# Rows taken from SBUF by one-hot products: two of 16 columns, in bf16, instead of one in f32

## The chip, the cores and the metric

One core of one Trainium2 chip runs the kernel. The metric is the device time of one execution in microseconds. The engines named below are TensorE (PE; PEld are its weight loads), VectorE (DVE), ScalarE (ACT), GpSimd (POOL), SyncE (SP) and the DMA engines.

## The reference

Four graph layers run over the same 6,250 nodes of 128 features and the same 100,000 edges (`src`, `dst`, sorted by `dst`), with `x = layernorm(x + layer(x))` after each:

```
L0: xl = x@W_lin + b; alpha = edge softmax over src of leaky(s_i[src] + s_j[dst]); sum over dst of alpha * xl[src]
L1: sum over dst of edge_weight * x[src]; out = x + sum; relu(out@W1 + b1)@W2 + b2
L2: per (edge type, dst) softmax of 4 scores, averaged; sum over dst of attn * (x[src] @ W_r[type]); layernorm, relu
L3: h = x@W; edge softmax over dst of leaky(s_src[src] + s_dst[dst]), own loops; sum over dst of alpha * h[src]
```

What matters here is the step that all four share: for every edge, fetch the row of its source node, weigh it, and add it up by target.

## The kernel before

Edges are padded to 128 x 784: each of the 128 partitions owns 784 consecutive edges ("columns"). A node's row lives at partition p, block b (node = 50p + b, `NB` = 50 blocks). Each layer has one **pass** over the 784 columns: layers 0, 1 and 2 in `sum_strands` (name prefixes l0z, l1z, l2z), layer 3 in `sum_messages` (l3z). A pass is cut into 48 full turns of 16 columns and two half turns of 8. For a turn:

- POOL issues one indirect DMA for each column (line 1103, line 927 in layer 3); it fetches 128 rows from the table in DRAM into `rows`, a ring of six turns (`RING`). The list of row numbers, `idx`, is in SBUF. POOL waits for `weighed` of six turns before.
- One column of each full turn in layers 0, 1 and 3 isn't fetched but **picked** (class `Picks`). PE makes the source numbers of the column into a row that all partitions see (`pcode`, in PSUM, line 822). DVE compares it with the names of a partition's nodes (`pnames`, in SBUF), and writes f32 one-hot matrices, one of 128x128 for each of the 50 blocks (line 813, in two or three parts). PE multiplies each with the node rows in SBUF and sums over the 50 blocks in `pfound` (line 836). ACT copies the result into `rows` (line 847). Everything about a pick is done one turn ahead: DVE marks the next turn's pick at the head of a turn.
- DVE then waits for the turn's DMAs and for its pick, weighs the rows into `msg`, and adds them up step by step, each step waiting for the last: four steps of two tensor operations (lines 1068 and 1069) in layers 0 to 2, 16 steps of one operation (line 899) in layer 3.
- SP stores the running sums to `prefix` in DRAM.

`Residual0` is extra DVE work in turns 20 to 32 of layer 0. Between passes stand the tails (`tail0` to `tail3`): POOL fetches 50 x 128 sums from `prefix`, DVE and ACT normalize them, SP writes the next table. Several operands of DVE (`keep`, `kept`, `factors`, `pcode`, `msg` in layer 3) are in PSUM, so that its frequent operations have one input in SBUF and one in PSUM.

The order of work on each engine is written out by hand; semaphores carry it from engine to engine.

```
WIDTH, RING, ACCS = 16, 6, 2
self.nc.vector.tensor_tensor(self.hot[i][:, 0:hi - lo], bc_mid(self.code[:], hi - lo), bc_last(self.names[:, lo:hi], P), ALU.is_equal)
mm = self.nc.tensor.matmul(self.found[:], self.hot[i][:, b - lo], self.nodes[:, b], start=b == 0, stop=b == NB - 1)
```

Of the kernel before, what the change touches and what calls it, by code (L numbers as in the profile page):

```python
# [755 lines left out]
WIDTH, RING, ACCS = 16, 6, 2  # L756
# [4 lines left out]


# [19 lines left out]
def halved(hot):  # L782
    return [hot[:, 0:NB // 2], hot[:, NB // 2:NB]]


class Picks:
# [3 lines left out]
    def __init__(self, nc, s, g, nodes, hot, columns):  # L790
        self.nc, self.g, self.nodes, self.hot, self.columns = nc, g, nodes, hot, columns
        self.count, self.parts, at = len(columns), [], 0
        for piece in hot:
            self.parts.append((at, min(at + piece.shape[1], NB)))
            at += piece.shape[1]
        self.base, self.names = s.sb("pbase", [P, 1]), s.sb("pnames", [P, NB])
        self.code, self.found = s.ps("pcode", [P, P]), s.ps("pfound", [P, nodes.shape[2]])
        self.coded, self.hotted, self.summed, self.placed = (s.sem("p" + n) for n in ("coded", "hotted", "summed", "placed"))

    def start(self, chain):  # L800
        v = self.nc.vector
        chain(v.tensor_scalar(self.base[:], self.g.part[:], float(NB), None, ALU.mult))
        chain(v.tensor_scalar(self.names[:], self.g.iota[:, 0:NB], self.base[:, 0:1], None, ALU.add))

    def on_vector(self, eng, k):
        if k >= self.count:
            return
        eng.wait_ge(self.coded, k + 1)
        n = len(self.parts)
        for i, (lo, hi) in enumerate(self.parts):  # L810
            if k:
                eng.wait_ge(self.summed, n * (k - 1) + i + 1)
            self.nc.vector.tensor_tensor(self.hot[i][:, 0:hi - lo], bc_mid(self.code[:], hi - lo), bc_last(self.names[:, lo:hi], P),  # L813
                                         ALU.is_equal).then_inc(self.hotted, 1)

    def landed(self, eng, k):
        if k < self.count:
            eng.wait_ge(self.placed, k + 1)

    def name(self, k):  # L820
        j = self.columns[k]
        self.nc.tensor.matmul(self.code[:], self.g.src[:, j:j + 1].to_broadcast([P, P]), self.g.ident[:],  # L822
                              start=True, stop=True).then_inc(self.coded, 1)

    def on_tensor(self, pe, k):
        if k >= self.count:
            return
        if k == 0:
            self.name(0)
        else:  # L830
            pe.wait_ge(self.placed, k)
        n = len(self.parts)
        for i, (lo, hi) in enumerate(self.parts):
            pe.wait_ge(self.hotted, n * k + i + 1)
            for b in range(lo, hi):
                mm = self.nc.tensor.matmul(self.found[:], self.hot[i][:, b - lo], self.nodes[:, b], start=b == 0, stop=b == NB - 1)  # L836
            mm.then_inc(self.summed, 1)
        if k + 1 < self.count:
            self.name(k + 1)

    def on_scalar(self, act, k, slot, weighed):
        if k >= self.count:
            return
        act.wait_ge(self.summed, len(self.parts) * (k + 1))
        if k >= RING:
            act.wait_ge(weighed, k - RING + 1)
        self.nc.scalar.copy(slot, self.found[:]).then_inc(self.placed, 1)


def sum_messages(nc, name, g, order, table, prefix, width, weigh, aside, spot):  # L850


    with Space(nc, name) as s:
# [11 lines left out]
        picks = Picks(nc, s, g, *spot, [hi - 1 for lo, hi in BATCHES if hi - lo == WIDTH])  # L865

        def landed(k):
            return 16 * sum(BATCHES[m][1] - BATCHES[m][0] - (m < picks.count) for m in range(k % RING, k + 1, RING))
# [6 lines left out]
        with s.block() as block:  # L875
            @block.vector
            def _(eng):
# [6 lines left out]
                picks.on_vector(eng, 0)  # L884
                for k, (lo, hi) in enumerate(BATCHES):
                    c = k % ACCS
                    aside.on_vector(eng, chain, k)
                    picks.on_vector(eng, k + 1)
# [16 lines left out]
            @block.tensor  # L905
            def _(pe):
                for k in range(len(BATCHES)):
                    picks.on_tensor(pe, k)
                    aside.on_tensor(pe, k)

            @block.scalar
            def _(act):
                picks.on_scalar(act, 0, rows[:, 0, WIDTH - 1], weighed)
                for k, (lo, hi) in enumerate(BATCHES):
                    aside.on_scalar(act, k)
                    w.on_scalar(act, k, hi - lo)
                    picks.on_scalar(act, k + 1, rows[:, (k + 1) % RING, WIDTH - 1], weighed)

            @block.gpsimd
            def _(pool):  # L920
                pool.wait_ge(indexed, 1)
                for k, (lo, hi) in enumerate(BATCHES):
# [3 lines left out]
                    for u in range(hi - lo - (k < picks.count)):  # L926
# [66 lines left out]
STRIDE = NC // STRANDS  # L993
ABREAST = WIDTH // STRANDS
# [16 lines left out]
def sum_strands(nc, name, g, order, table, prefix, width, weigh, aside, spot=None, acc=None):  # L1011
# [3 lines left out]
    with Space(nc, name) as s:  # L1015
        rows = s.sb("rows", [P, RING, WIDTH, width])
        msg = s.sb("msg", [P, WIDTH, D])
        acc = s.sb("acc", [P, ACCS, WIDTH, D])[:] if acc is None else acc
        keep, kept = s.ps("keep", [P, STRIDE, STRANDS]), s.ps("kept", [P, STRANDS, D])
# [6 lines left out]
        w = weigh(nc, s, us, es, weighed, rows, msg)  # L1026
        full = sum(hi - lo == ABREAST for lo, hi in TURNS)
        picks = Picks(nc, s, g, *spot, [(STRANDS - 1) * STRIDE + TURNS[k][1] - 1 for k in range(full)]) if spot else None

        def picked(k):  # L1030
            return 1 if picks and k < picks.count else 0
# [8 lines left out]
        with s.block() as block:  # L1040
            @block.vector
            def _(eng):
# [4 lines left out]
                chain(v.tensor_copy(keep[:], by_step(order.keep[:])))  # L1047
                last = by_strand(acc[:, ACCS - 1])[:, :, ABREAST - 1]
                if picks:
                    picks.start(chain)  # L1050
                    picks.on_vector(eng, 0)
                for k, (lo, hi) in enumerate(TURNS):
                    aside.on_vector(eng, chain, k)
                    if picks:
                        picks.on_vector(eng, k + 1)
# [8 lines left out]
                    for u in range(hi - lo):  # L1064
                        if lo + u:
                            eng.wait_ge(summed, lo + u)
                        here = sums(k)[:, :, u]
                        chain(v.tensor_tensor(kept[:], last, bc_last(keep[:, lo + u], D), ALU.mult))
                        v.tensor_tensor(here, kept[:], by_strand(msg[:, 0:STRANDS * (hi - lo)])[:, :, u], ALU.add).then_inc(summed, 1)
                        last = here  # L1070
                eng.wait_ge(summed, STRIDE)
# [3 lines left out]
            def _(pe):  # L1075
                for k in range(len(TURNS)):
                    if picks:
                        picks.on_tensor(pe, k)
                    aside.on_tensor(pe, k)

            @block.scalar
            def _(act):
                if picks:
                    picks.on_scalar(act, 0, rows[:, 0, WIDTH - 1], weighed)
                for k, (lo, hi) in enumerate(TURNS):
                    aside.on_scalar(act, k)
                    w.on_scalar(act, k, STRANDS * (hi - lo))
# [1711 lines left out]
```

## Time and profile before

| | us |
|---|---|
| median of 3 runs | 6681.86 (6681.67 to 6683.09) |
| span of the profiled execution | 6678.7 |
| pass of layer 0: first gather to last operation of DVE | 1370.3 to 2297 |
| pass of layer 1 | 2389.1 to 3312 |
| pass of layer 2 | 4453.7 to 5460 |
| pass of layer 3 | 5628.3 to 6551 |

The span leaves 3.2 us to the median. "Busy" is the time in which an engine ran an instruction; for PE the ends are modelled, so the pace is read from counts in a window. An f32 matmul shows as two records on PE and two on PEld. PEclk is the granted TensorE clock as a share of 2.4 GHz; its two levels are 1.2 and 2.4 GHz.

### The profile page before, as it was taken

The numbers are of one execution on the slowest core, as the hardware profiler recorded it, in microseconds if no ns is written. First come the engines' busy times: TensorE is split into PE (matmuls) and PEld (weight loads), VectorE is DVE, ScalarE is ACT, GpSimd is POOL, SyncE is SP. The second block draws the span as 40 slices with busy tenths as digits, with TensorE's granted clock in tenths as the row PEclk, the third lists the DMA queues.
The fourth block names the chain that finished last, engine by engine and source line by source line (L and its number), as shares of the span: only waits on it lengthen the run. The fifth ranks groups of instructions, "written<-read, shape, count | busy, mean of one in ns | idle before, by whom it ended". The sixth has DMA issues, their size and how long they took to land. (4 is left out here: it accounts for less than half of the span.)

```text
span 6678.7 us, 61345 instructions
## 1 busy us (share of the span) xinstructions
PE 3332.5 (50%) x21638; PEld 2959.0 (44%) x21638; DVE 5046.5 (76%) x7174; ACT 1003.4 (15%) x2297; POOL 4583.7 (69%) x4753
## 2 busy tenths in 40 slices
PE   7530117467777457777468857730000004777770
PEld 5530106357777457777443327730000003777770
DVE  8999998778898677787647779986343446888886
ACT  1013333200000010000034435520000003000002
POOL 0027777677777677777667777777777767777774
PEclk9999558788989778888779988865555556888885
DMA  3036011134444344444339974433343332333332
GB/s 60 1 148 256 2 32 18 26 85 115 115 112 113 101 115 110 110 110 110 99 124 345 343 283 122 126 88 107 103 108 104 103 92 59 112 112 112 112 112 71
DMA packets 588107, 763.09 MB, mean 114 GB/s; under 512 B 118267, under 2 KB 479585, under 8 KB 568345
## 3 DMA queue, kind: packets, MB, share of 16 engines
q1 hardware_dynamic: 416916, 375.57, 17.7%
q0 software_dynamic: 152672, 272.57, 17.1%
q10 hardware_dynamic: 18210, 111.02, 4.2%
q8 instruction: 171, 2.80, 0.2%
q14 instruction: 138, 1.13, 0.1%
HBM read 346.63 MB, written 412.16 MB: 114 GB/s over the span
## 5 line engine op out<-in xcount | busy, mean ns | idle before, releaser
L1103 POOL DMA_INDIRECT l2z_rows<-proj,l2z_idx x784 | 764.5, 975 | 246.2 <-issue 238.6
L2685 POOL DMA_INDIRECT l2s_krow<-table_k,l2s_idx x762 | 721.8, 947 | 232.2 <-issue 230.4
L1103 POOL DMA_INDIRECT l0z_rows<-table,l0z_idx x736 | 697.3, 947 | 234.7 <-issue 224.0
L927 POOL DMA_INDIRECT l3z_rows<-table,l3z_idx x736 | 694.6, 944 | 234.7 <-issue 224.0
L1103 POOL DMA_INDIRECT l1z_rows<-table,l1z_idx x736 | 694.6, 944 | 233.5 <-issue 213.0
L836 PE MATMUL l3z_pfound<-l3h_hn,l3h_hot 128*128 128x130 f32 x4800 | 645.1, 303 | 233.9 <-DVE l3h_hot L813 233.9
L836 PE MATMUL l1z_pfound<-g_x,l2o_xT 128*128 128x128 f32 x4800 | 638.3, 303 | 238.9 <-DVE l2o_xT L813 238.9
L836 PEld LDWEIGHTS l3z_pfound<-l3h_hn,l3h_hot 128*128 128x128 f32 x4800 | 637.2, 218 | 241.8 <-issue 234.7
L836 PEld LDWEIGHTS l1z_pfound<-g_x,l2o_xT 128*128 128x128 f32 x4800 | 630.5, 218 | 246.6 <-issue 239.0
L2097 POOL DMA_INDIRECT first_sj<-scores,first_atdst x504 | 504.7, 1001 | 170.7 <-issue 170.7
L836 PE MATMUL l0z_pfound<-first_rows,l0r_hot 128*128 128x140 f32 x3648 | 468.0, 292 | 82.0 <-DVE l0r_hot L813 81.9
L836 PEld LDWEIGHTS l0z_pfound<-first_rows,l0r_hot 128*128 128x128 f32 x3648 | 458.0, 197 | 92.9 <-DVE l0r_hot L813 92.9
L1136 DVE TENSOR_TENSOR l2z_msg<-l2z_rows,l2z_factors 128x1024 f32<-128x1024 f32 (+1 forms) x50 | 60.0, 1200 | 511.5 <-DMA l2z_rows<-proj,l2z_idx 511.0
L2643 PE MATMUL l2s_bank<-l2o_wr,l2o_xT 128*128 128x512 f32 x800 | 373.5, 622 | 98.0 <-ACT l2s_proj L2657 83.2
L813 DVE TENSOR_TENSOR l2o_xT<-l1z_pcode,l1z_pnames 128x3200 f32<-128x3200 f32 x96 | 330.3, 3481 | 20.8 <-PE l1z_pcode L822 20.7
L813 DVE TENSOR_TENSOR l3h_hot<-l3z_pcode,l3z_pnames 128x3200 f32<-128x3200 f32 x96 | 330.4, 3483 | 12.8 <-PE l3z_pcode L822 12.5
L606 POOL IOTA sd_nidi<- 128x50 int32 x1 | 0.2, 170 | 429.8 <-POOLq L60 429.8
L2643 PEld LDWEIGHTS l2s_bank<-l2o_wr,l2o_xT 128*128 128x128 f32 x800 | 153.5, 197 | 317.7 <-issue 167.9
L899 DVE SCALAR_TENSOR_TENSOR l3z_acc<-l3z_acc,l3z_xx,l3z_msg 128x128 f32<-128x128 f32 x784 | 271.8, 347 | 25.9
L2541 PE MATMUL l2s_bank<-l2o_kn,l2o_xT 128*128 128x128 f32 x2200 | 286.2, 299 | 5.3 <-DVE l2o_xT L2522 5.3
L2541 PEld LDWEIGHTS l2s_bank<-l2o_kn,l2o_xT 128*128 128x128 f32 x2200 | 286.3, 216 | 5.5 <-issue 5.5
L268 PE MATMUL sd_turn<-g_ident,prep_key 128*128 128x128 f32 x112 | 27.5, 428 | 493.0 <-DVE prep_key L245 487.7
(619 smaller groups left out, 7639.4 us busy)
## 6 DMA issues: line engine op xcount, KB each, us to landing
proj<-l2s_proj ACTq DMA_DIRECT2D x100, 1024.0 KB
spread_q<-prep_zero SPq DMA_DIRECT2D x98, 656.0 KB
l2s_zrow<-spread_q SPq DMA_DIRECT2D x98, 656.0 KB, 4.8
prefix<-l0z_acc SPq DMA_DIRECT2D x196, 256.0 KB, 3.1
prefix<-l2o_kn SPq DMA_DIRECT2D x196, 256.0 KB
prefix<-l2z_acc SPq DMA_DIRECT2D x196, 256.0 KB
prefix<-l3z_acc SPq DMA_DIRECT2D x48, 1040.0 KB, 4.1
l2z_rows<-proj,l2z_idx POOLq DMA_INDIRECT x784, 2.6
```

Of the source, the lines that this page charges most:

```text
L268: mm = self.nc.tensor.transpose(self.turn[q][:, u], self.keys[at % 2][:, c:c + P], self.g.ident[:])
L606: nc.gpsimd.iota(nid_i[:], pattern=[[1, NB]], base=EP, channel_multiplier=NB).then_inc(numbered, 1)
L813: self.nc.vector.tensor_tensor(self.hot[i][:, 0:hi - lo], bc_mid(self.code[:], hi - lo), bc_last(self.names[:, lo:hi], P), ALU.is_equal).t ...
L836: mm = self.nc.tensor.matmul(self.found[:], self.hot[i][:, b - lo], self.nodes[:, b], start=b == 0, stop=b == NB - 1)
L899: v.scalar_tensor_tensor(acc[:, c, u, 0:D], sum_before(k, u)[:, 0:D], w.factor(k, lo, u), msg[:, u], ALU.mult, ALU.add).then_inc(summed, 1)
L927: nc.gpsimd.indirect_dma_start(out=rows[:, k % RING, u, :], out_offset=None, in_=table, in_offset=bass.IndirectOffsetOnAxis(ap=idx[:, lo + ...
L1103: nc.gpsimd.indirect_dma_start(out=rows[:, k % RING, c * (hi - lo) + u, :], out_offset=None, in_=table, in_offset=bass.IndirectOffsetOnAxi ...
L1136: chain.add(self.v.tensor_tensor(msg[:, 0:half], rows[:, 0:half], bc_last3(factor[:, 0:half], D), ALU.mult))
L2097: nc.gpsimd.indirect_dma_start(out=sj[:, j, :], out_offset=None, in_=g.scores0, in_offset=bass.IndirectOffsetOnAxis(ap=at_dst[:, j:j + 1], ...
L2541: mm = self.nc.tensor.matmul(self.found, self.hot[:, b], self.nodes[:, b], start=b == 0, stop=b == NB - 1)
L2643: mm = nc.tensor.matmul(bank[m % 2][:, b], xT[:, i, :], wr[:, c:c + wide], start=True, stop=True)
L2685: nc.gpsimd.indirect_dma_start(out=krow[:, k % KRING, c * (hi - lo) + u, :], out_offset=None, in_=g.table_k, in_offset=bass.IndirectOffset ...
```

## The change

- In layers 0, 1 and 3 two columns of each full turn, and one of each half turn, are picked: 98 picks in a pass in place of 48, and 686 gathers in place of 736.
- Node rows are held as three bf16 pieces whose sum is the f32 row exactly: the high piece is read in place from the f32 rows (every second bf16), the middle and low piece are made by DVE into a new tile `ml` (class `Pieces`: three DVE operations for each group of blocks). For layer 0 that is done ahead of the pass (`first`, five times ten blocks), for layers 1 and 3 inside `tail0` and `tail2`.
- The one-hot matrices are bf16. ACT turns the row of source numbers into a row of block numbers in bf16 in SBUF (`digit`), and DVE compares `digit` with `blocks` (SBUF, bf16). Parts: two of 25 blocks, in layer 0 four of 12 or 13 blocks. A ring holds four parts (six in layer 0: three reused areas and three new).
- For each block PE runs three bf16 products with the same one-hot matrix. `pfound` is doubled. Everything about picks is two turns ahead (`AHEAD`), and DVE's marks are spread over a turn in five shares, between the steps of the sum.
- `RING` goes from six to four turns, in layer 2 too. `keep`, `kept` and the factors are packed in one PSUM area; `keep` leaves out the last eight steps, which read the copy in SBUF.

```diff
-WIDTH, RING, ACCS = 16, 6, 2
+WIDTH, RING, ACCS, PICKED = 16, 4, 2, 2
+class Pieces:
+    def make(self, chain, b):
+        v, x, rest, ml = self.nc.vector, self.nodes[:, b], self.rest[:, 0:b.stop - b.start], self.ml[:, b]
+        chain(v.tensor_tensor(rest, x, x.bitcast(BF16)[:, :, 1::2], ALU.subtract))
+        chain(v.tensor_copy(ml[:, :, 0], rest.bitcast(BF16)[:, :, 1::2]))
+        chain(v.tensor_tensor(ml[:, :, 1], rest, ml[:, :, 0], ALU.subtract))
+AHEAD = 2
+SHARES = 5
 class Picks:
...
+    def mark(self, eng, at):
+        n, i = at // self.parts, at % self.parts
+        lo, hi = self.cuts[i], self.cuts[i + 1]
+        if i == 0:
+            eng.wait_ge(self.dug, n + 1)
+        if at >= len(self.hot):
+            eng.wait_ge(self.summed, at - len(self.hot) + 1)
+        out = self.hot[at % len(self.hot)].rearrange("p b (r q) -> p b r q", q=16)
+        names = self.blocks[:, lo:hi].unsqueeze(2).to_broadcast([P, hi - lo, P // 16, 16])
+        digit = self.digit[:, n % 2].rearrange("p (r q) -> p r q", q=16).unsqueeze(1).to_broadcast([P, hi - lo, P // 16, 16])
+        self.nc.vector.tensor_tensor(out, names, digit, ALU.is_equal).then_inc(self.hotted, 1)
+    def on_vector(self, eng, k, share):
+        todo = self.of(k + AHEAD)
+        lo, m = todo.start * self.parts, len(todo) * self.parts
+        for at in range(lo + m * share // SHARES, lo + m * (share + 1) // SHARES):
+            self.mark(eng, at)
...
+                for b in range(self.cuts[i], self.cuts[i + 1]):
+                    hot = self.hot[at % len(self.hot)][:, b - self.cuts[i]]
+                    t.matmul(found, hot, high[:, b, 1::2], start=b == 0, stop=False)
+                    t.matmul(found, hot, self.ml[:, b, 0], start=False, stop=False)
+                    mm = t.matmul(found, hot, self.ml[:, b, 1], start=False, stop=b == NB - 1)
+                mm.then_inc(self.summed, 1)
+    def dig(self, act, n):
+        if n == 0:
+            act.wait_ge(self.based, 1)
+        act.wait_ge(self.coded, n + 1)
+        if n >= 2:
+            act.wait_ge(self.hotted, self.parts * (n - 1))
+        self.nc.scalar.activation(self.digit[:, n % 2], self.code, ACT.Identity, bias=self.base[:, 0:1]).then_inc(self.dug, 1)
...
                     for u in range(hi - lo):
+                        if picks:
+                            picks.on_vector(eng, k, 1 + u)
...
+    def first(self, chain):
+        for b in range(0, NB, 10):
+            self.pieces.make(chain, slice(b, b + 10))
...
+                    if i >= 2:
+                        eng.wait_ge(normed, GROUPS[i - 2][-1] + 1)
+                        pieces.make(chain, span(GROUPS[i - 2]))
...
+                    j = i - 5
+                    if j >= 0:
+                        eng.wait_ge(ready, GROUPS[j][-1] + 1)
+                        pieces.make(chain, span(GROUPS[j]))
```

## Rows read from the trace of the kernel before

**Rows 1.** The page, part 1: busy us, share of span, instructions of each engine.
```profile
PE 3332.5 (50%) x21638; PEld 2959.0 (44%) x21638; DVE 5046.5 (76%) x7174; ACT 1003.4 (15%) x2297; POOL 4583.7 (69%) x4753
```
**Rows 2.** Busy time in windows: PE, PEld, DVE, ACT, POOL, then PEclk; passes 0, 1, 3.
```profile
1370.30:2288.30 918.00, 679.87 (x4894) 661.13 (x4894) 779.46 (x855) 25.79 (x97) 694.64 (x734) 0.89 0.46 113
2389.10:3307.90 918.80, 649.90 (x4904) 642.17 (x4904) 720.01 (x595) 12.94 (x49) 694.54 (x736) 0.86 0.41 111
5628.30:6546.00 917.70, 655.50 (x4894) 647.70 (x4894) 769.98 (x1320) 29.84 (x147) 693.68 (x736) 0.86 0.38 110
```
**Rows 3.** The page, part 5: busy us, mean ns | idle before, and its cause; layer 1.
```profile
L1103 POOL DMA_INDIRECT l1z_rows<-table,l1z_idx x736 | 694.6, 944 | 233.5 <-issue 213.0
L836 PE MATMUL l1z_pfound<-g_x,l2o_xT 128*128 128x128 f32 x4800 | 638.3, 303 | 238.9 <-DVE l2o_xT L813 238.9
L813 DVE TENSOR_TENSOR l2o_xT<-l1z_pcode,l1z_pnames 128x3200 f32<-128x3200 f32 x96 | 330.3, 3481 | 20.8 <-PE l1z_pcode L822 20.7
```
**Rows 4.** Groups by line and shape, columns as in rows 3.
```profile
L813 DVE TENSOR_TENSOR l0r_hot<-l0z_pcode,l0z_pnames 128x4864 f32<-128x4864 f32 x48 | 250.3, 5214 | 0.0
...
L1068 DVE TENSOR_TENSOR l1z_kept<-l2o_kn,l1z_keep 128x512 f32<-128x512 f32 x196 | 136.3, 695 | 10.2 <-issue 0.9
...
L899 DVE SCALAR_TENSOR_TENSOR l3z_acc<-l3z_acc,l3z_xx,l3z_msg 128x128 f32<-128x128 f32 x784 | 271.8, 347 | 25.9
...
L337 DVE TENSOR_TENSOR sa_toh<-prep_steps,sa_thib 128x2048 bf16<-128x2048 bf16 x49 | 59.9, 1222 | 4.3 <-PE sa_ttally L346 4.3
...
L338 DVE TENSOR_TENSOR sa_tol<-prep_steps,sa_tlob 128x800 bf16<-128x800 bf16 x49 | 27.9, 570 | 0.0
```
**Rows 5.** Waits in passes 0, 1, 3: us in total, times, longest.
```profile
DVE l0z_a L1159 <- DMA l0z_rows<-table,l0z_idx: 80.2, 41, 9.1
DVE l1z_msg L1136 <- DMA l1z_rows<-table,l1z_idx: 158.3, 44, 10.2
DVE l3z_e L974 <- DMA l3z_rows<-table,l3z_idx: 86.6, 43, 8.7
```
**Rows 6.** Bursts of line 836 (layers 3, 0) and line 346: PE, PEld records, PEclk.
```profile
5911.00:5918.00 7.00, 7.00 (x65) 7.00 (x65) 0.00 (x0) 1.00 0.26 55
1803.00:1811.00 8.00, 8.00 (x69) 8.00 (x69) 0.00 (x0) 1.00 0.33 83
200.20:203.20 3.00, 3.00 (x31) 3.00 (x31) 1.00 0.00 0
```
**Rows 7.** Windows of line 268, f32 transposes: PE, PEld busy (x records), PEclk.
```profile
640.00:750.00 110.00, 9.84 (x40) 7.84 (x40) 0.52 0.06 2
116.00:420.00 304.00, 25.59 (x104) 20.39 (x104) 1.00 0.08 1
```
**Rows 8.** Timeline at the start of pass 1: start us, us, engine, line.
```profile
2392.74 6.89 DVE L813 TENSOR_TENSOR l2o_xT<-l1z_pcode,l1z_pnames 128x3200 f32<-128x3200 f32 x2
2392.82 0.94 POOL L1103 DMA_INDIRECT l1z_rows<-table,l1z_idx  x1 [0.30 <-issue]
```
**Rows 9.** Timeline of layer 2's pass and of the sort's end, columns as in rows 8.
```profile
4476.70 3.42 DVE L2428 TENSOR_TENSOR l2b_bwd<-l_qv,l_attn 128x3136 f32<-128x3136 f32 x1
4477.79 3.15 POOL L1103 DMA_INDIRECT l2z_rows<-proj,l2z_idx  x1 [0.30 <-issue]
...
1025.10 7.08 DVE L2133 TENSOR_TENSOR_SCAN sd_si<-first_sokeep,sd_init,sd_si 128x784 f32<-128x784 f32 x4
...
1028.01 1.44 POOL L2097 DMA_INDIRECT first_sj<-scores,first_atdst  x1 [0.30 <-issue]
1029.76 1.44 POOL L2097 DMA_INDIRECT first_sj<-scores,first_atdst  x1 [0.30 <-issue]
```
**Rows 10.** Windows of tail 0 and tail 2, columns as in rows 2.
```profile
2297.00:2389.00 92.00, 2.98 (x10) 1.94 (x10) 40.42 (x113) 25.80 (x114) 55.59 (x58) 0.50 0.27 83
5460.00:5625.00 165.00, 39.41 (x158) 33.24 (x158) 93.91 (x243) 68.71 (x290) 113.34 (x109) 0.54 0.18 52
```

More of the change, by code:

```diff
@@ L779, in on_tensor, with slots @@
         pass
-def halved(hot):
-    return [hot[:, 0:NB // 2], hot[:, NB // 2:NB]]
-class Picks:
[L790 to L798, printed above, removed]
+def slots(flat, sizes):
+    out, at = [], 0
+    for n in sizes:
+        out.append(flat[:, at:at + n * P].rearrange("p (b q) -> p b q", q=P))
+        at += n * P
+    return out
@@ new lines, with __init__, picked, of @@
+AHEAD = 2
+BANK = 512
+SHARES = 5
+class Picks:
+    def __init__(self, nc, s, g, spot, todo, weighed):
+        self.nc, self.g, self.weighed = nc, g, weighed
+        self.nodes, self.ml, self.hot, self.cuts = spot
+        self.columns = [j for batch in todo for j, _ in batch]
+        self.slots = [u for batch in todo for _, u in batch]
+        self.first = [sum(len(batch) for batch in todo[:k]) for k in range(len(todo) + 1)]
+        self.count, self.parts, self.width = len(self.columns), len(self.cuts) - 1, self.nodes.shape[2]
+        self.base, self.blocks = s.sb("pbase", [P, 1]), s.sb("pblocks", [P, NB, 16], BF16)
+        self.digit = s.sb("pdigit", [P, 2, P], BF16)
+        self.code = s.ps("pcode", [P, BANK])[:, 0:P]
+        self.found = [s.ps(f"pfound{h}", [P, BANK])[:, 0:self.width] for h in range(2)]
+        self.based, self.coded, self.dug, self.hotted, self.summed, self.placed = (
+            s.sem("p" + n) for n in ("based", "coded", "dug", "hotted", "summed", "placed"))
+    def picked(self, k):
+        return self.first[k + 1] - self.first[k]
+    def of(self, k):
+        last = len(self.first) - 1
+        return range(self.first[max(0, min(k, last))], self.first[max(0, min(k + 1, last))])
@@ L816, in landed @@
-    def landed(self, eng, k):
[L817 to L822, printed above, removed]
+        chain(v.tensor_copy(self.blocks[:], bc_last(self.g.iota[:, 0:NB], 16)))
+        v.tensor_scalar(self.base[:], self.g.part[:], -float(NB), None, ALU.mult).then_inc(self.based, 1)
+    def mark(self, eng, at):
[9 more added lines that the diff above has]
+        self.nc.vector.tensor_tensor(out, names, digit, ALU.is_equal).then_inc(self.hotted, 1)
@@ L825, in on_tensor @@
     def on_tensor(self, pe, k):
[L826 to L837, printed above, removed]
@@ L925, in _ @@
                         hold(pool, weighed, k - RING + 1)
-                    for u in range(hi - lo - (k < picks.count)):
+                    for u in range(hi - lo - picks.picked(k)):
                         nc.gpsimd.indirect_dma_start(out=rows[:, k % RING, u, :], out_offset=None, in_=table,
@@ L1025, in sum_strands @@
         stored = [s.sem(f"sto{r}") for r in range(ACCS)]
-        w = weigh(nc, s, us, es, weighed, rows, msg)
-        full = sum(hi - lo == ABREAST for lo, hi in TURNS)
-        picks = Picks(nc, s, g, *spot, [(STRANDS - 1) * STRIDE + TURNS[k][1] - 1 for k in range(full)]) if spot else None
+        w = weigh(nc, s, us, es, weighed, rows, msg, room[:, 4 * BANK - NC:])
+        todo = [[((STRANDS - 1) * STRIDE + hi - 1 - i, STRANDS * (hi - lo) - 1 - i) for i in range(STRANDS * (hi - lo) * PICKED // WIDTH)]
+                for lo, hi in TURNS]
+        picks = Picks(nc, s, g, spot, todo, weighed) if spot else None
         def picked(k):
-            return 1 if picks and k < picks.count else 0
+            return picks.picked(k) if picks else 0
         def landed(k):
```

176 lines of the change are left out of this document (112 added, 64 removed).

## The prediction

> **What bounds the kernel now.** First the page's busy line [rows 1]: no engine is full, so the passes are read one by one. In each of the passes 0, 1 and 3 POOL is busy 694 of 918 us [rows 2], and what is left of it is nearly all "issue" [rows 3]: it waits for nobody. Its pace is the bound: 918.8 us for 735 intervals is 1.250 us for a gather. DVE waits for the gathers' DMAs for 80, 158 and 87 us in passes 0, 1 and 3 [rows 5]; so it is occupied for 838, 760 and 831 us of 918 and is a close second. PE is busy for 650 to 680 us [rows 2] and waits for marks. A full turn takes 15 gathers, 18.75 us. The changed passes gain if POOL keeps its pace with fewer gathers and DVE and PE keep up.
>
> **What is removed.** 50 gathers in each of three passes: 50 x 1.250 = 62.5 us each, 187 us in all, if POOL still sets the end. POOL's pass would be 686 x 1.250 = 857 us.
>
> **DVE's marks.** A mark was f32, 3481 ns for 3200 elements [rows 3], 5214 for 4864 [rows 4]; so 96 marks in passes 1 and 3 (330 us), and 48 x 7.1 = 341 us in pass 0. The nearest rows for a bf16 mark are two bf16 comparisons, both inputs in SBUF, 1222 ns for 2048 elements and 570 for 800 [rows 4]: 0.522 ns an element and 152 ns fixed. 3200 elements are 1.82 us, 1600 (12 or 13 blocks) 0.99. Pass 1 and 3: 196 x 1.82 = 357, +27 us. Pass 0: 392 x 0.99 = 388, +47. DVE's occupation becomes 885, 787 and 858 us in passes 0, 1, 3: level with POOL's 857 in layer 3, above it in layer 0. If the two repeated inputs cost the mode that gives 0.522, the f32 price holds: +352 us in each of passes 1 and 3 and some +370 in pass 0.
>
> **PE's products.** A pick was 50 f32 products, two record pairs each: 65 pairs in 7.00 us in layer 3 (108 ns a pair), 69 in 8.00 in layer 0 (116 ns, 140 columns), PEclk 1.00 [rows 6]. A pair takes as long as 256 columns at 2.4 GHz (107 ns), so the weight load is hidden there. A bf16 product passes its columns once; half a pair is 55 ns, in layer 0 59 ns. A pick is 150 x 55 = 8.25 us plus 0.4 for name and hand-over (two pairs, and as much again), and 98 picks are 848 us; in layer 0 98 x 9.25 = 907. PE runs nearly without pause, so I keep the 2.4 GHz level for it. This is the lower bound: the load must hide under 53 ns of columns instead of 107. The only bf16 products of the trace, line 346, take 3.00 us for 31, 97 ns each with only 50 columns [rows 6]. Their clock column says 1.00, but f32 transposes in that same window take 25.59/104 = 0.246 us of busy time, and in a window at 0.52 also 9.84/40 = 0.246 [rows 7]: line 346 ran at the 1.2 GHz level, and its 50 columns are 42 of the 97 ns. If the remaining 55 ns is a load that can't be hidden, it is 28 ns at 2.4 GHz, or 55 if it doesn't scale: a product takes 82 or 109 ns. Taken: hidden, as in the f32 rows, which are the nearest in column count; those loads are also read with a stride, the new ones aren't.
>
> **What the marks do to POOL.** This is the step on which the forecast turns. The old mark has one input in PSUM (`pcode`) and one in SBUF; a gather issued 0.08 us after such a mark begins takes its 0.94 us [rows 8], and the means of 944 [rows 3] say that all do. The new mark has both inputs in SBUF (`digit`, `blocks`). Lines 2428 and 2133 are operations of DVE with two SBUF inputs. Line 2428 runs from 4476.70 to 4480.12; the same gather instruction begun inside it takes 3.15 us and ends at 4480.94, 0.82 us after it. Under four scans in 7.08 us the gathers follow each other at 1.75 us, one for each scan, not 1.25 [rows 9]. So a gather that begins under such an operation goes on only when it ends. No row shows it for a bf16 one; both bounds are kept: no stall, or this one.
> The Trainium skill, "SBUF — State Buffer", section "Who interferes with whom", says that a DVE instruction with two SBUF inputs contends with a GpSimd instruction that reads SBUF. By that rule the trace agrees, in 3.15 us against 0.94, and it makes no exception for bf16.
>
> **Turn by turn, with the stall.** In layer 1 a mark of 1.82 is followed by one step (two operations of 0.69 to 0.70 [rows 4] and their gaps, 1.45), then the next mark. A gather is released when a mark ends; one more follows 1.25 later, and the third, due at 2.50, meets the next mark, which began at 1.45, and is held until 3.27. Two gathers take 3.27 instead of 2.50: 0.77 lost for each of four marks, 3.1 us in a turn. The turn is 14 x 1.25 + 3.1 = 20.6 us against 18.75: +1.85 x 48 = +89 us. In layer 3 four steps of 0.347 [rows 4] with gaps are 1.5; the cycle is 3.34, the loss 0.84 x 4 = 3.4, the turn 20.9: +2.15 x 48 = +103. PE (17.3 us a turn) and DVE (16.1 and 17.5) are hidden under both. In layer 0 eight marks of 0.99 each meet a gather with 0.99/1.25 chance and hold it half a mark, 0.39 us: 3.1 us a turn at most (20.6, +89), and near nothing where the held gather falls into step, since one goes through between two marks. I take the middle for POOL, below 18.75 to 19; then PE's 907 us decides, and behind it the start: `first` puts 15 operations of 1400 elements (1.6 us each by the f32 slope) ahead of the first mark, 23 us. 907 + 23 + some 16 for the last turns' sums is 946 against 926: +20. In turns 20 to 32 DVE's residual rows come on top (1.4 us), beside PE.
>
> **Tails.** `make` adds three operations to each of 13 groups in `tail0` and `tail2`, 1.4 to 2.1 us a group, 18 to 27 us each. DVE is busy 40 of 92 us in tail 0 and 94 of 165 in tail 2 [rows 10], so most is hidden; the last groups trail, and two of the three operations have two SBUF inputs and hold gathers. I take +6 and +12, between 0 and 27 each.
>
> **At nothing.** ACT's moves of digits and rows: ACT is busy 13 to 30 us of a pass [rows 2]; without that slack each would cost some 0.3 us. The smaller ring: POOL's idle time before a gather is its usual 0.3 us throughout [rows 3], and DVE stays within a turn of it; in layer 2's start DVE comes 94 us after POOL, about the time of 64 gathers with their stalls (bounds 0 and +10). SP's stores are unchanged in number.
>
> **Sum.** 89 + 103 + 20 + 18 = +230 us on 6678.7. The median of the runs is 3.2 above the span; against it: 6682 + 230 = 6912 us.
>
> **Rivals.**
> *Gathers aren't held* (bf16 marks leave POOL alone). Passes 1 and 3 follow POOL and DVE: -62 and -55; layer 0 +20, tails +18: 6603 us, faster. For it: no bf16 row in contact with POOL. Against it: every row with two SBUF inputs. It decides when the loss of a turn falls under 1.25 us, what one gather less gives.
> *Weight loads aren't hidden* (82 ns). 98 x (150 x 0.082 + 0.4) = 1245 us in passes 1 and 3, 98 x (150 x 0.087 + 0.4) = 1318 in pass 0: +327, +327, +400, tails +18: 7750 us. PE then sets the end and POOL's stalls are hidden. It decides from 66 ns on (turns of 20.6). For it line 346, against it the f32 pairs. At 109 ns it would be near 8900.
> The Trainium skill, "TensorE: Matmul & The Clock Gate", section "Back-to-back issue gap", gives about 81 ns for a matmul of 128 columns in a stream of loads and matmuls, and 56 for one by itself. By the first this rival's sum would stand at about the same place; no run so far shows it.
> *Marks at the f32 price.* Passes 1 and 3 at DVE's 1113 and 1183 us, pass 0 at 1210: about 7450.
> *No change*: a shorter stall and a smaller gain meet, 6670 to 6695.
>
> **Chances.** Forecast (gathers held, loads hidden) 0.50; gathers not held 0.20; loads not hidden 0.20; marks at the f32 price 0.04; no change or between 0.06. The forecast's own range is 6850 to 7010 (tails 0 to 54 for 18, layer 0's POOL up to +89). Leaving out either of the larger rivals leaves out over 2 in 10 with the forecast's own tails, so the range takes in both: 6590 to 7760. A time within 0.2% (13 us) is about what a measurement can't tell from no change. Faster 0.21, same 0.04, slower 0.75.
>
> **What would show it.** Mean of a gather in l1z and l3z: 1.15 to 1.2 us if held (3.1 us over 14), 0.94 if not. DVE's marks: 1.82 and 0.99 us. PE's records of line 836 in a burst: 55 to 59 ns apart, or 82. DVE's wait for gathers in pass 1 stays large if POOL sets the end; if PE does, DVE and ACT wait for `pfound` and marks. Wrong would be: gathers at 0.94 with PE at 55 (then it is faster), or turns of 25 us.

## The result, and the profile after

The changed kernel takes 6887.65 us (median of 4 runs, 6883.4 to 6892.2) against 6681.76 for the kernel before beside it; the ratio is 1.0309, 95% interval 1.0297 to 1.0322. It is 206 us slower; the forecast was 230 us slower. The profiled execution has a span of 6881.5 us, 202.8 more than before.

Where the time went is read from the first gather of each pass (first starts of the tiles `l0z_rows` to `l3z_rows`): before 1370.3, 2389.1, 4453.7, 5628.3, end 6678.7; after 1368.6, 2438.0, 4570.1, 5746.8, end 6881.5. So the stretch of pass 0 and tail 0 grew by 50.6 us, pass 1 with what follows by 67.5, pass 2 with tail 2 by 2.1, pass 3 with the end by 84.3, and the start is 1.7 shorter: 202.8.

The page after, part 1; its answer before is [rows 1].
```profile
PE 4117.3 (60%) x51638; PEld 3751.8 (55%) x51638; DVE 5134.1 (75%) x7715; ACT 1129.8 (16%) x2741; POOL 4829.2 (70%) x4603
```
POOL has 150 instructions fewer and is busy for 246 us more. For the gathers that is the story in one line: the work that was taken away from POOL comes back as longer instructions.

Windows of the changed kernel, with the columns of [rows 2]: passes 0, 1, 3, then tails 0 and 2 (those of before are in [rows 10]).
```profile
1368.50:2343.20 974.70, 941.44 (x14894) 939.79 (x14894) 825.96 (x1131) 68.94 (x246) 756.15 (x686) 0.98 0.40 105
2437.90:3430.50 992.60, 894.10 (x14904) 886.40 (x14904) 725.66 (x701) 56.99 (x197) 777.97 (x687) 0.95 0.35 101
5746.70:6757.60 1010.90, 919.54 (x14895) 912.01 (x14894) 778.03 (x1439) 68.72 (x297) 793.00 (x686) 0.96 0.34 98
2343.20:2437.90 94.70, 2.99 (x10) 1.96 (x10) 59.59 (x148) 25.81 (x114) 56.41 (x58) 0.50 0.26 78
5581.20:5746.80 165.60, 40.36 (x160) 33.82 (x160) 114.08 (x278) 68.83 (x290) 114.75 (x109) 0.52 0.17 51
```
In pass 0 PE is busy for 941 of 975 us: its products run from 1395.89 to 2335.95 almost without a pause, so it is full. In passes 1 and 3 it isn't, and POOL is busy for 80 to 100 us more than in [rows 2] with 50 gathers fewer.

Groups of the changed kernel, with the columns of [rows 3] (the old L1103 is L1194 now, L813 is L850, L836 is L884 to L886).
```profile
L999 POOL DMA_INDIRECT l3z_rows<-table,l3z_idx x686 | 793.0, 1156 | 219.5 <-issue 208.7
L1194 POOL DMA_INDIRECT l1z_rows<-table,l1z_idx x686 | 777.1, 1133 | 222.5 <-issue 208.4
L1194 POOL DMA_INDIRECT l0z_rows<-table,l0z_idx x686 | 756.1, 1102 | 219.5 <-issue 208.4
L1194 POOL DMA_INDIRECT l2z_rows<-proj,l2z_idx x784 | 766.2, 977 | 246.1 <-issue 238.5
...
L850 DVE TENSOR_TENSOR l2o_xT<-l1z_pblocks,l1z_pdigit 128x3200 bf16<-128x3200 bf16 x196 | 356.6, 1821 | 26.3 <-PE l1z_pfound L886 13.7 <-ACT l1z_pdigit L895 8.6
L850 DVE TENSOR_TENSOR l3h_hot<-l3z_pblocks,l3z_pdigit 128x3200 bf16<-128x3200 bf16 x196 | 355.5, 1815 | 14.9 <-PE l3z_pfound L886 14.2 <-ACT l3z_pdigit L895 0.4
L850 DVE TENSOR_TENSOR l0r_hot<-l0z_pblocks,l0z_pdigit 128x1664 bf16<-128x1664 bf16 x196 | 200.3, 1022 | 105.5 <-PE l0z_pfound L886 101.0 <-issue 0.4
```
The mean gather was 944 ns in [rows 3]; it is 1133, 1156 and 1102 ns in the changed passes and nearly unchanged in layer 2, which has no marks. The idle time before a gather is still "issue", 0.30 us: POOL still waits for nobody, each gather lasts longer. The marks cost what was forecast, 1.82 us for 3200 elements and 1.02 for 1664 (by the forecast's slope 1.02).

How one gather becomes longer: the timeline of layer 1 in mid-pass (start us, us, engine, line; PE's rows left out).
```profile
2899.25 0.95 POOL L1194 DMA_INDIRECT l1z_rows<-table,l1z_idx  x1 [0.30 <-issue]
2899.38 1.81 DVE L850 TENSOR_TENSOR l2o_xT<-l1z_pblocks,l1z_pdigit 128x3200 bf16<-128x3200 bf16 x1
...
2900.51 1.51 POOL L1194 DMA_INDIRECT l1z_rows<-table,l1z_idx  x1 [0.30 <-issue]
...
2901.11 0.69 DVE L1149 TENSOR_TENSOR l1z_room<-l2o_kn,l1z_room 128x512 f32<-128x512 f32 x1
...
2902.32 0.94 POOL L1194 DMA_INDIRECT l1z_rows<-table,l1z_idx  x1 [0.30 <-issue]
...
2902.44 1.81 DVE L850 TENSOR_TENSOR l2o_xT<-l1z_pblocks,l1z_pdigit 128x3200 bf16<-128x3200 bf16 x1
```
The gather at 2899.25 begins 0.13 us ahead of a mark and takes its usual 0.95. The next, at 2900.51, begins under the mark, which ends at 2901.19; the gather ends at 2902.02, 0.83 after it. Compare [rows 8], where a gather under an f32 mark takes 0.94; in pass 1 of the kernel before, 250 gathers begin under an f32 mark, over 0.15 us ahead of its end, and none takes more than 0.95. It is no single case: in pass 3 of the changed kernel 197 of 686 gathers begin under a mark in this sense, and 196 of them end 0.81 to 0.83 us after the mark. The one left begins 0.02 us after the mark's start and takes 0.95.

### The profile page after: what moved, and what is told of

Its sections match the earlier page's. It is cut to its first block and busy times, and to the rows that moved or that the text cites. A ratio compares the mean times of both kernels' runs of the same rounds, so it can differ in the third digit from the quotient of the medians.

```text
span 6881.5 us, 122899 instructions
## 1 busy us (share of the span) xinstructions
PE 4117.3 (60%) x51638; PEld 3751.8 (55%) x51638; DVE 5134.1 (75%) x7715; ACT 1129.8 (16%) x2741; POOL 4829.2 (70%) x4603
## 5 line engine op out<-in xcount | busy, mean ns | idle before, releaser
L999 POOL DMA_INDIRECT l3z_rows<-table,l3z_idx x686 | 793.0, 1156 | 219.5 <-issue 208.7
L1194 POOL DMA_INDIRECT l2z_rows<-proj,l2z_idx x784 | 766.2, 977 | 246.1 <-issue 238.5
L1194 POOL DMA_INDIRECT l1z_rows<-table,l1z_idx x686 | 777.1, 1133 | 222.5 <-issue 208.4
L884 PE MATMUL l3z_pfound<-l3h_hn,l3h_hot 128*128 128x130 bf16 x4900 | 888.2, 224 | 74.8 <-DVE l3h_hot L850 74.6
L884 PE MATMUL l1z_pfound<-g_x,l2o_xT 128*128 128x128 bf16 x4900 | 861.9, 223 | 82.8 <-DVE l2o_xT L850 82.7
L1194 POOL DMA_INDIRECT l0z_rows<-table,l0z_idx x686 | 756.1, 1102 | 219.5 <-issue 208.4
L886 PE MATMUL l3z_pfound<-l3h_ml,l3h_hot 128*128 128x130 bf16 x4900 | 887.4, 224 | 0.0
L885 PE MATMUL l3z_pfound<-l3h_ml,l3h_hot 128*128 128x130 bf16 x4900 | 887.1, 222 | 0.0
L886 PE MATMUL l1z_pfound<-l1m_ml,l2o_xT 128*128 128x128 bf16 x4900 | 861.3, 222 | 0.0
L885 PE MATMUL l1z_pfound<-l1m_ml,l2o_xT 128*128 128x128 bf16 x4900 | 860.7, 221 | 0.0
L884 PEld LDWEIGHTS l3z_pfound<-l3h_hn,l3h_hot 128*128 128x128 bf16 x4900 | 490.0, 100 | 79.7 <-issue 74.2
L884 PEld LDWEIGHTS l1z_pfound<-g_x,l2o_xT 128*128 128x128 bf16 x4900 | 483.8, 99 | 89.0 <-issue 83.3
L885 PEld LDWEIGHTS l1z_pfound<-l1m_ml,l2o_xT 128*128 128x128 bf16 x4900 | 487.9, 100 | 0.7
L886 PE MATMUL l0z_pfound<-l0r_ml,l0r_hot 128*128 128x140 bf16 x2548 | 482.2, 225 | 0.0
L884 PE MATMUL l0z_pfound<-first_rows,l0r_hot 128*128 128x140 bf16 x2548 | 482.0, 224 | 0.0
L885 PE MATMUL l0z_pfound<-l0r_ml,l0r_hot 128*128 128x140 bf16 x2548 | 481.7, 222 | 0.0
L886 PEld LDWEIGHTS l1z_pfound<-l1m_ml,l2o_xT 128*128 128x128 bf16 x4900 | 480.2, 98 | 0.0
L885 PEld LDWEIGHTS l3z_pfound<-l3h_ml,l3h_hot 128*128 128x128 bf16 x4900 | 479.7, 98 | 0.8
L886 PEld LDWEIGHTS l3z_pfound<-l3h_ml,l3h_hot 128*128 128x128 bf16 x4900 | 479.3, 98 | 0.0
```

The source lines that it names most:

```text
L884: t.matmul(found, hot, high[:, b, 1::2], start=b == 0, stop=False)
L885: t.matmul(found, hot, self.ml[:, b, 0], start=False, stop=False)
L886: mm = t.matmul(found, hot, self.ml[:, b, 1], start=False, stop=b == NB - 1)
L999: nc.gpsimd.indirect_dma_start(out=rows[:, k % RING, u, :], out_offset=None, in_=table, in_offset=bass.IndirectOffsetOnAxis(ap=idx[:, lo + ...
L1194: nc.gpsimd.indirect_dma_start(out=rows[:, k % RING, c * (hi - lo) + u, :], out_offset=None, in_=table, in_offset=bass.IndirectOffsetOnAxi ...
```

## Experiments

The theory, H: a gather that begins under a mark is held until the mark's end + 0.82 us; this sets the end of passes 1 and 3, and PE's 300 products a turn set that of pass 0. The rival, L: PE's rows, twice as many as before and with a ring of 4, come late, DVE waits, and the long gather records are a symptom that costs nothing. For L spoke that DVE's wait for rows in pass 1 had grown from 158 us [rows 5] to 233, and PE's load from 650 to 894 us. Four kernels (one pick, thin marks, one product, marks placed by the rule) ran beside a kernel before of 6680.7 us (median); the other three (one input and the two with layer 0 as before) ran on another chip, beside one of 6689.0. The first four of the kernels below ran once each, so their totals have no interval.

**One pick instead of two.**
```diff
-WIDTH, RING, ACCS, PICKED = 16, 4, 2, 2
+WIDTH, RING, ACCS, PICKED = 16, 4, 2, 1
```


> The changed kernel with one pick a turn instead of two (15 gathers, two marks and 150 products in a turn of passes 1 and 3; four marks in pass 0). Theory H, gathers are held by marks: a mark alone between steps lets the gather that begins u after its start end at its own end + 0.82, so it costs 1.81 + 0.82 - 0.94 - u, with u from 0 to 1.25: 0.44 to 1.69, in the mean 1.06. A turn is 15 x 1.25 + 2 x 1.06 = 20.9 us (19.6 to 22.1), the gathers of pass 1 take 960 to 1080 us from first to last against 987 with two picks, although PE has half the work; mean gather 1.0 to 1.15 us. Rival L, late rows: with two picks, 300 products a turn and a ring of 4, rows from PE come late and the long gather records are a symptom; with half of PE's work passes 1 and 3 return to 919 us. Pass 0: PE falls from 940 to 470 us; its gathers take 930 to 1000 us by H, 920 by L.

It took 6909.2 us. The gathers of pass 1 took 984.2 us from first to last, those of pass 3 1003.1 (987.0 and 1001.7 with two picks), those of pass 0 996.8 (964.9 with two). PE has about half the products (7200 a pass instead of 14700), and yet the gathers of pass 1 are only 3 us shorter and those of the other passes are longer. Two marks that stand alone cost (1031 - 944) x 15 = 1.3 us a turn in layer 1 and (1059 - 944) x 15 = 1.7 in layer 3: inside the bounds of two times 0.44 to 1.69, and under the mean of 2.1. L falls for passes 1 and 3. With these losses the two settings tie in layer 1: 14 x 1.25 + 2.6 = 20.1 us a turn with four marks, 15 x 1.25 + 1.3 = 20.1 with two.

**Thin marks.** Only the first block of each part is compared, after one round of full marks; the kernel leaves out the rest of the one-hot matrices, so its picked rows have no meaning:
```diff
-        lo, hi = self.cuts[i], self.cuts[i + 1]
+        lo, hi = self.cuts[i], self.cuts[i + 1] if at < len(self.hot) else self.cuts[i] + 1
...
-        out = self.hot[at % len(self.hot)].rearrange("p b (r q) -> p b r q", q=16)
+        out = self.hot[at % len(self.hot)][:, 0:hi - lo].rearrange("p b (r q) -> p b r q", q=16)
```


> The changed kernel with marks of one block (128 elements, about 0.22 us) instead of 25 or 12 to 13, after the first round of full ones: most of the marks is left out, PE's products, ACT's moves and the gathers all stay. H: the mean gather goes back to 0.94 to 0.96 us and POOL to 857 us; then PE sets the end of passes 1 and 3: 98 picks of 150 x 57.9 ns = 8.7 us are 851 us and with hand-over 865 to 885 in pass 1, 150 x 60.4 ns = 9.06 us are 888 and with hand-over 890 to 910 in pass 3 (987 and 1002 with full marks). Pass 0 stays at PE's 940 us and some 30 more. In all about 6680 us. L: PE's work and the ring are unchanged, so passes 1 and 3 stay within 15 us of 987 and 1002, about 6870 us.

It took 6646.6 us; the expectation's total of about 6680 was 33 us too high, and its 865 to 885 and 890 to 910 us for passes 1 and 3 were met at the low ends. Windows of its passes 0, 1 and 3:
```profile
1369.20:2343.30 974.10, 941.74 (x14894) 940.08 (x14894) 549.96 (x1131) 70.32 (x246) 659.91 (x686) 0.98 0.41 105
2438.20:3303.00 864.80, 855.74 (x14862) 853.87 (x14862) 427.01 (x695) 56.58 (x196) 651.39 (x687) 0.99 0.43 116
5623.40:6520.50 897.10, 886.17 (x14894) 884.47 (x14894) 483.94 (x1439) 74.24 (x297) 649.59 (x686) 0.99 0.38 111
```
The gathers of pass 1 take 860.5 us and their mean is 948 ns. The account closes: (1133 - 948) ns x 686 = 127 us, and pass 1's gathers were 987.0 - 860.5 = 126.5 us longer with full marks; in pass 3 (1156 - 947) x 686 = 143.4 against 143.3. These windows also give PE's own time, where it is hardly held up by marks: 855.7 us in pass 1, 886.2 in pass 3 and 941.7 in pass 0, where the forecast had 848, 848 and 907. Pass 0 stays at 974 us. This run alone doesn't tell a held gather from a DVE that has 300 us less to do; the one with one input, below, does.

**One product for each block.**
```diff
-                    t.matmul(found, hot, high[:, b, 1::2], start=b == 0, stop=False)
-                    t.matmul(found, hot, self.ml[:, b, 0], start=False, stop=False)
-                    mm = t.matmul(found, hot, self.ml[:, b, 1], start=False, stop=b == NB - 1)
+                    mm = t.matmul(found, hot, high[:, b, 1::2], start=b == 0, stop=b == NB - 1)
```


> The changed kernel with one product for each block instead of three: the second and third pieces are left out of the sum, the marks, the moves and the gathers stay. H: passes 1 and 3 stay within 15 us of 987 and 1002 us, mean gather 1.13 to 1.16 us, since POOL and the marks are as they were. L: PE has a third of its work (290 us a pass) and rows are never late, so passes 1 and 3 fall to 857 to 900 us. Pass 0: if PE's 63 ns a product set its end, it is shorter than 974.5 us, by 5 to 45 us, down to what POOL with its held gathers takes (14 x 1.25 + 1.75 to 3 us a turn, 943 to 1000 us, less the 12 us by which the sums trail at the end).

It took 6916.7 us, 29 more than with all three products. The gathers of pass 1 took 986.7 us and of pass 3 1009.8, as H has it. But pass 0 became longer, 1003.2 us against 974.7, with PE busy for 525 instead of 941; the expectation was missed. Its mean gather is 1147 ns, up from 1102. So in pass 0 two limits lie close together: with thin marks PE's 941 us give 974, and with PE relieved the held gathers give 1003. With both, the held gathers lose less than they do alone, and the time is 974.7. From start to start of every 14th gather, the turns of the changed kernel's layer 0 repeat at 19.17 us, with 1.7 us of holding in each, until the residual rows begin, and are then 20.4 us long for some ten turns; with one product they are mostly 20.1 to 20.4 us throughout. A likely reading is that PE's pace, to which DVE's marks are tied by their wait for PE (101 us in that pass), also fixes where the marks fall on the gathers. It is read from the trace and wasn't tried by itself, and each side is one run.

**One input.** The block names are compared with one number for each partition, so that the operation has one SBUF tensor; the kernel leaves the marks' meaning out:
```diff
-        self.nc.vector.tensor_tensor(out, names, digit, ALU.is_equal).then_inc(self.hotted, 1)
+        self.nc.vector.tensor_scalar(out, names, self.base[:, 0:1], None, ALU.is_equal).then_inc(self.hotted, 1)
```


> The changed kernel with each mark replaced by a comparison of the same bf16 block names with one number for each partition: same output size and place, one tensor from SBUF instead of two; the marks' meaning is left out. H in its narrow form, two SBUF inputs hold a gather: the mean gather in passes 1 and 3 goes back to 0.94 to 0.97 us and their length to PE's pace, as with thin marks: gathers of pass 1 860 to 880 us, of pass 3 860 to 900, in all about 6650 to 6700. Rival W, any fast bf16 operation of DVE holds gathers whatever its inputs: a gather that begins under such a mark still ends 0.82 us after it, and the passes stay over 900 us as far as the mark is not shorter than a gather (at 1.8 us a mark 987 and 1002 us, at 1 us a mark some 900 to 940).

It took 6656.2 us, and this is the run that decides. Groups of this kernel:
```profile
L1194 POOL DMA_INDIRECT l1z_rows<-table,l1z_idx x686 | 648.9, 946 | 222.6 <-issue 207.9 <-DVE l1z_idx L766 13.7 <-DVE l2o_kn L1228 0.9
L999 POOL DMA_INDIRECT l3z_rows<-table,l3z_idx x686 | 648.6, 945 | 219.6 <-issue 208.8 <-DVE l3z_idx L766 10.7
```
and its window of pass 1:
```profile
2438.20:3303.00 864.80, 855.15 (x14837) 852.94 (x14836) 735.98 (x692) 56.71 (x196) 649.83 (x687) 0.99 0.42 115
```
DVE is busy for 736 us, no less than the 726 of the changed kernel, each mark takes 1.88 us, and PE has all its products; still the gathers are at 946 ns and the pass at 865 us. So it is not the length of the marks, nor DVE's time, nor PE's load: what holds a gather goes with the second SBUF input. The narrow form of H stands for passes 1 and 3. The edit also turns a TENSOR_TENSOR into a TENSOR_SCALAR, and no run has a bf16 TENSOR_TENSOR with one SBUF input. That the operation by itself is the cause is made unlikely by the f32 marks, which are TENSOR_TENSOR with one input in SBUF and hold none of 250 gathers, and by the f32 operation with two SBUF inputs of [rows 9], which holds one.

Layer 0 adds something that neither side had. There the same instruction runs at two speeds, mostly 0.61 to 0.67 us for 12 blocks and 1.08 for 13, and the fast one does hold a gather though it has one input (timeline of the same kernel):
```profile
1469.53 0.61 DVE L850 TENSOR_SCALAR first_sokeep<-l0z_pblocks,l0z_pbase 128x1536 bf16<-128x1536 bf16 x1
1469.69 1.27 POOL L1194 DMA_INDIRECT l0z_rows<-table,l0z_idx  x1 [0.30 <-issue]
```
The mark ends at 1470.14, the gather at 1470.96, again 0.82 later. None of 133 gathers under a mark of 13 blocks ended by that rule.
The Trainium skill, "SBUF — State Buffer", section "Who interferes with whom", says both: a DVE instruction with two SBUF inputs contends with a GpSimd instruction that reads SBUF, and one that runs in a mode that uses both ports contends with GpSimd. With that rule this trace agrees, with 1.27 us against 0.94, if the fast marks run in such a mode; no row names the mode.

**Marks placed by the rule.** If H holds, its rule can be used. The comparisons stay the same, but six marks of 14 to 18 blocks take the place of four of 25, and most stand in groups: after a mark's end + 0.82 + 0.30 the next gather begins, and with a mark of 1.27 us behind the first it meets that one's end. The code takes a list of places in a turn for each layer (2 is ahead of the second step, 5 is behind the last):
```diff
-        lo, m = todo.start * self.parts, len(todo) * self.parts
-        for at in range(lo + m * share // SHARES, lo + m * (share + 1) // SHARES):
-            self.mark(eng, at)
+        for i, at in enumerate(range(todo.start * self.parts, todo.stop * self.parts)):
+            if self.place[i] == share:
+                self.mark(eng, at)
...
+CUTS1, PLACE1 = (0, 18, 36, 50), (2, 2, 3, 5, 5, 5)
+CUTS3, PLACE3 = (0, 18, 34, 50), (2, 2, 3, 3, 3, 4)
```


> The changed kernel with the same marks cut and placed otherwise in layers 1 and 3: six marks a turn of 14 to 18 blocks (1.1 to 1.35 us) instead of four of 25 (1.82 us), in groups with nothing between them, so that a gather released at a mark's end + 0.82 and followed 0.30 later by the next one meets the end of the following mark and not its start. Same comparisons, products and gathers in all. H: a group costs its first gather up to 1.2 us and nearly nothing after; turns of 18.2 to 18.8 us in layer 1 and 18.0 to 18.6 in layer 3 instead of 20.1 and 20.4, gathers of pass 1 890 to 925 us, of pass 3 885 to 915; in all 6690 to 6750 us. L, or a loss that goes with the marks' total time: passes 1 and 3 stay at 987 and 1002 us or grow by the fixed part of two more marks a turn (0.15 us each), 6885 to 6910 us.

It took 6703.2 us (9 runs, ratio to before 1.0031, 1.0021 to 1.0041): 184 us less than the changed kernel, with the same products, gathers and compared elements. Gathers of pass 1 took 895.4 us (mean 999 ns), of pass 3 913.8 (1028). A group of three marks with the gathers beside it:
```profile
2917.56 0.94 POOL L1194 DMA_INDIRECT l1z_rows<-table,l1z_idx  x1 [0.30 <-issue]
...
2917.73 3.62 DVE L850 TENSOR_TENSOR l2o_xT<-l1z_pblocks,l1z_pdigit 128x2304 bf16<-128x2304 bf16 x3
...
2918.81 1.08 POOL L1194 DMA_INDIRECT l1z_rows<-table,l1z_idx  x1 [0.30 <-issue]
2920.20 0.96 POOL L1194 DMA_INDIRECT l1z_rows<-table,l1z_idx  x1 [0.30 <-issue]
2921.47 0.94 POOL L1194 DMA_INDIRECT l1z_rows<-table,l1z_idx  x1 [0.31 <-issue]
```
These three marks, 3.6 us of two-input work, cost POOL 0.16 us, where the mark of 25 blocks shown above cost 0.57. They are a good case: by the means, six marks cost (999 - 944) x 14 = 0.8 us a turn in layer 1 and (1028 - 944) x 14 = 1.2 in layer 3, where four of 25 blocks cost 2.6 and 3.0. Length and place were changed together, so the runs don't say how much each gave.

**Layer 0 as before.** The old class with its f32 marks is kept for layer 0 alone:
```diff
-        picks = Picks(nc, s, g, spot, todo, weighed) if spot else None
+        if spot and len(spot) == 2:
+            picks = Picks0(nc, s, g, spot, [turn[0][0] for turn in todo if len(turn) == PICKED], weighed)
+        else:
+            picks = Picks(nc, s, g, spot, todo, weighed) if spot else None
```


> The changed kernel with layer 0 as before (one f32 pick a turn, no pieces made ahead of it, but the ring of 4); layers 1 and 3 keep the change. The trace says that layer 0 is 45 us longer with the change, 21 of it for the pieces made ahead of the first mark. If that is additive: 6888 - 45 = 6843 us (6836 to 6850), pass 0 929 us from first gather to last sum, passes 1 and 3 unchanged at 987 and 1002. If the smaller ring cost pass 0 something it stays above 935.

Pass 0 took 930.0 us: its 45 us are given back, and the ring of 4 costs nothing there. But the time was 6863.9 us (4 runs, 6851.1 to 6868.5; ratio 1.0256, 1.0241 to 1.0272), 175 us above the kernel before where 206 - 45 = 161 was expected. The rest is in pass 1, whose code is that of the changed kernel and whose gathers took 1005.5 us (mean 1160) instead of 987.0, while pass 3 took 1003.4. The turns of pass 1 have two common lengths, 19.7 and 20.8 us from start to start of every 14th gather; in the changed kernel 27 of 48 are of the short kind and 9 of the long one, here 10 and 23. What pass 1 loses thus depends on how marks and gathers happen to fall on each other; some 20 us either way aren't in the code of the pass. Why the shares differ is open.

**Both.** Layer 0 as before, layer 1 as placed above, layer 3 with cuts (0, 16, 33, 50) and places (1, 1, 2, 2, 3, 3).

> Layer 0 as before, and in layers 1 and 3 the change with six smaller marks a turn; layer 1 placed as in the run before it (gathers 895 us), layer 3 with marks of 16, 17 and 17 blocks in three pairs ahead of the first, second and third group of steps instead of (2, 3, 1). H: with the rule (a gather begun under a mark ends at the mark's end + 0.82, the next begins 0.30 later) a layer 3 turn comes to 17.6 us for POOL, below PE's 18.1: gathers of pass 3 870 to 895 us against 914 in the run before, whole pass with the last sums 895 to 910. In all 6703 - 45 - 20 = 6638 us (6620 to 6660), faster than the kernel before by 0.3 to 0.9%. L, or a loss that goes with the marks' total time: pass 3 stays at 914 or more, 6655 to 6665 us.

It took 6650.2 us (5 runs, 6649.2 to 6653.5) against 6689.0; ratio 0.9942, 95% interval 0.9929 to 0.9956: faster than the kernel before by 0.6% and, by the two ratios, than the changed one by 3.6%. Groups and the window of pass 3:
```profile
L1072 POOL DMA_INDIRECT l3z_rows<-table,l3z_idx x686 | 685.7, 1000 | 219.6 <-issue 208.8 <-DVE l3z_idx L766 10.7
L1270 POOL DMA_INDIRECT l1z_rows<-table,l1z_idx x686 | 685.5, 999 | 222.6 <-issue 208.6 <-DVE l1z_idx L766 13.7 <-DVE l2o_kn L1304 0.3
```
```profile
5617.60:6523.10 905.50, 887.11 (x14895) 885.31 (x14894) 792.98 (x1537) 74.46 (x297) 685.72 (x686) 0.99 0.36 110
```
Pass 3 is 905 us with PE busy for 887, as long as with thin marks (886): now PE is the bound there. Its gathers took 894.5 us, at the upper end of the expectation. The total lies inside the expected 6620 to 6660.

## Why the prediction was right, point by point

**The bound.** POOL's pace set passes 1 and 3 before and sets them now; its idle time before a gather is "issue" in both. The gain that was counted, 62.5 us for 50 gathers, is real where nothing is held: with thin marks and with one input the 686 gathers take 857 to 861 us, as the forecast had it (857).

**The held gathers**, the step on which the forecast turned, were right, and the mechanism is shown by the run with one input. The sizes were too high. A turn loses (1133 - 944) x 14 = 2.6 us in layer 1 and 3.0 in layer 3, where 3.1 and 3.4 were forecast; that is 15% too much in a turn, and as the gain from one gather less is taken off it, more in the growth: pass 1 grew by 67 us instead of 89, pass 3 by 84 instead of 103. The term that was off is the time between marks: I added a mark's 1.82 us to a step of 1.45 and got 3.27. In the trace marks follow at 2899.38 and 2902.44, 3.06 us apart, since the step's first record begins 0.08 us ahead of the mark's end (2901.11 against 2901.19), and the next mark as much ahead of the step's. Two gathers for 3.06 us lose 0.56, not 0.77. In layer 3 marks follow each other mostly at 3.13 to 3.14 us, where 3.34 was forecast. The first mark of a turn costs up to 1.6 us (a gather of 2.52 us at 2912.87), which gave back part of that.

**The marks' price** was right: 1.82 us for 25 blocks, and 0.95 and 1.02 for 12 and 13, against 1.82 and 0.99. The marks of pass 0 grew from 341.5 to 387.7 us in all, 46 (forecast 47), and those of pass 1 from 330.3 us [rows 3] to 356.6, the 26 to 27 of the forecast.

**PE.** That loads stay hidden was right: products of one burst follow each other at 55 to 63 ns (medians 55, 59 and 63 in layers 1, 3 and 0), not at 82. The size was off: 98 picks took 941 us in pass 0, where 907 was forecast, and need 856 and 886 us in passes 1 and 3 (thin marks) where 848 was. The rows of [rows 6] gave 116 ns for an f32 pair of 140 columns from a count of records in 8 us, so 59 for a bf16 product counted in half pairs; in pass 0 it is 941 us / 14894 records = 63 ns, 4 more. In layer 3 I took layer 1's 55, where it is 59 or 60. The Trainium skill, "TensorE: Matmul & The Clock Gate", section "Back-to-back issue gap", has about 81 ns for 128 columns in such a stream; this trace disagrees, with a median of 55 ns from start to start in layer 1. In passes 1 and 3 nothing hung on the size. In pass 0, where PE sets the end, it is 34 us: the mis-sized term behind the +20 that came out as +45.

**Layer 0's start** was right: the 15 operations of `first` run from 1371.71 to 1392.83, 21 us (forecast 23), and they push PE's first product, on which that pass hangs. That PE sets the end of this pass was right as well: its products take 940 us from the first to the last, with full marks and with thin ones. But my reason for it, POOL below 18.75 to 19 us a turn, was wrong: with PE relieved POOL's turns are mostly 20.1 us and more, and the pass takes 1003. The middle value for its holding was too low, and the full 20.6 us a turn (1009 us) was nearer. In the changed kernel the gathers lost less beside a busy PE, which the forecast didn't foresee; so far as it goes, that is luck.

**Tails.** Tail 0, from the last sum to the next gather, grew from 89.7 to 94.9 us: +5, forecast +6. Tail 2 grew by 0.5, so its term of +12 was wrong: its window holds 20 us more of DVE's work [rows 10], all of it beside other work.

**At nothing.** The smaller ring: pass 0 with the old marks and the ring of 4 takes 930 us against 929, and pass 2 grew by 1.5 us. ACT's moves were not tried by themselves; the thin marks keep them all, and passes 1 and 3 then end with PE.

**The rivals.** "Gathers aren't held" forecast 6603 us; the kernel with one input, in which they aren't, took 6656, more because PE's 941 and 886 us then set passes 0 and 3. "Weight loads aren't hidden" fell by the 55 to 63 ns between products, "marks at the f32 price" by the 1.82 us of a mark.

**The sum.** 67 + 84 + 45 + 5 + 2 = 203 us in the profiled execution. The forecast had 89 + 103 + 20 + 18 = 230. Passes 1 and 3 and the tails were 22, 19 and 12 us too high, layer 0 was 25 too low and the rest about right, so that 53 us of errors one way met 25 the other way. The direction and the mechanism are the forecast's merit; that the total came within 24 us of the runs is in part luck, as pass 1 alone moved by 18 us between two kernels with the same code for it. The stated range, 6590 to 7760 us, took in all the larger rivals, so a time inside it decides nothing between them. What decides is the mean gather (1133 and 1156 ns where 1150 to 1200 was forecast, and about 940 by the rival), the price of a mark and the pace of PE.

## What to carry to other kernels

Before work is moved to a faster form on DVE, look at what the form does to GpSimd: an operation with two SBUF inputs held nearly every indirect gather that began under it (196 of 197 in pass 3) until its own end + 0.82 us. In pass 1 this cost 127 us, about twice the 62.5 us of the 50 gathers that the change took away. If such an operation must run beside a stream of gathers, its total alone doesn't set the loss, its length and place count too: cut to about one gather's interval (1.25 us) and set in groups, the same comparisons cost 92 us less in pass 1 and 107 in pass 3. Take intervals from start to start in a timeline; a sum of durations overstated the cycle by 0.2 us in 3.

## What the runs showed of the hardware that was not expected

- Relieving the engine that was the bound made a pass slower: one product instead of three, PE busy 525 instead of 941 us, pass 0 at 1003 instead of 975 us. That a bound elsewhere can keep marks and gathers in a good phase is the likely reason, and isn't shown.
- The one-input bf16 comparison ran at two speeds by its number of blocks, 0.61 to 0.67 us for most of 12 and 1.08 for 13, and only the faster one held gathers.
- A gather that begins about 0.1 us ahead of a two-input mark isn't held at all (2899.25 and 2899.38, 0.95 us). The order of start decides, but for a small margin: of 209 gathers that began under a mark in pass 1, the 13 that weren't held began within 0.04 us of the mark's start, and the 196 others more than 0.04 us after it.
- PE's bf16 products with f32 accumulation ran at 57.6 ns for 128 columns (855.74 us for 14862 records), 59.5 for 130 and 63.2 for 140: loads hidden, with 4 to 5 ns over the columns' own time at the 2.4 GHz level, which the clock column of 0.98 to 0.99 names.
